# First feed-forward of a two-layer block: gates spread by DMA through DRAM instead of by matmul, and the front of a pair two pairs ahead

## The reference, cut to what matters

```python
xn = _layernorm(x)
gates = softmax(xt @ Wg.T)                       # 16 experts
scores, inds = top_k(gates, 2); scores /= scores.sum()
g = einsum('td,ehd->teh', xt, We_gate)           # 64 hidden rows per expert
u = einsum('td,ehd->teh', xt, We_up)
h = silu(g) * u
y = sum over the 2 chosen experts of scores * (h @ We_down)
shared = silu(xt @ Ws_gate.T) * (xt @ Ws_up.T) @ Ws_down.T   # 256 hidden rows
y = y + sigmoid(xt @ Wsg.T) * shared
```

## Time and profile before

| | before |
|---|---|
| device time, median of 3 runs | 2905.8 us (2904.94 to 2909.46) |
| device time of the profiled execution | 2909.2 us |
| span of the profiled execution | 2907.5 us |
| busy over the span: PE, DVE, ACT, POOL | 90%, 66%, 55%, 21% |
| feed-forward of layer 0, first hidden matmul to last PE work | 42.69 to 554.04 us (the last down matmuls start at 549.92 and take 4.12) |
| mean granted TensorE clock | 0.969 |

### The profile page before, as it was taken

The page is one execution under the profiler, slowest core; times in us unless marked ns, Lnnn a source line. Parts: engine busy times, 40 slices in busy tenths (PEclk is TensorE's granted clock), DMA queues, the critical chain, the costliest instruction groups (busy, mean ns, idle before and its releaser), DMA issues. The chain is left out here.

```text
span 2907.5 us, 102728 instructions
## 1 busy us (share of the span) xinstructions
PE 2604.1 (90%) x42000; PEld 1971.0 (68%) x42000; DVE 1924.4 (66%) x7310; ACT 1611.4 (55%) x3731; POOL 613.6 (21%) x632
## 2 busy tenths in 40 slices
PE   4999999799988999999999999499989999998998
PEld 3777777567767777777777777377766666666666
DVE  4887788467777777777777777211117777777777
ACT  1444444366666666666666665133327666767776
POOL 2445444300110000001111111400004223322230
PEclk9999999899999999999999999699999999999999
DMA  3212100166666666666666665222321001111110
GB/s 131 103 51 73 37 15 12 36 152 148 154 151 149 152 153 148 152 155 149 152 150 153 150 149 123 86 84 98 101 72 35 24 24 29 26 24 24 28 27 9
DMA packets 341502, 268.43 MB, mean 92 GB/s; under 512 B 24602, under 2 KB 328090, under 8 KB 339516
## 3 DMA queue, kind: packets, MB, share of 16 engines
q1 hardware_dynamic: 330556, 234.82, 31.4%
q0 software_dynamic: 10496, 27.28, 3.2%
HBM read 129.88 MB, written 132.14 MB: 90 GB/s over the span
## 5 line engine op out<-in xcount | busy, mean ns | idle before, releaser
L869 DVE CUSTOM_DVE_ANT_0 neg_scores<-scores,rel_bias 128x256 f32<-128x256 f32 x1024 | 373.4, 421 | 271.7 <-PE scores L1013 226.4
L1388 ACT ACTIVATE probs<-neg_scores,low 128x256 f32<-128x256 f32 (+1 forms) x1024 | 382.5, 446 | 211.6 <-DVE low L1419 187.4
L757 ACT ACTIVATE probs<-neg_scores,low 128x256 f32<-128x256 f32 x1024 | 436.8, 500 | 42.9 <-DVE low L869 41.8
L751 ACT COPY probsT_s<-probsT 128x512 f32<-128x512 f32 x256 | 150.3, 587 | 427.6 <-PE probsT L1025 427.6
L1419 DVE CUSTOM_DVE_ANT_0 neg_scores<-scores,alibi 128x256 f32<-128x256 f32 (+1 forms) x1024 | 304.8, 354 | 109.5 <-PE scores L1466 109.2
L1025 PE MATMUL probsT<-consts,probs 128*128 128x128 f32 x2048 | 332.7, 286 | 1.3 <-ACT probsT_s L751 0.7
L1025 PEld LDWEIGHTS probsT<-consts,probs 128*128 128x128 f32 x2048 | 229.1, 143 | 72.9 <-issue 59.4
L252 POOL TENSOR_TENSOR hid<-hid,gate_bc 128x512 f32<-128x512 f32 x160 | 205.4, 1284 | 275.8 <-DVE hid L407 257.3
L876 DVE COPY rel_s<-scores 128x768 f32<-128x768 f32 x256 | 244.0, 953 | 3.0 <-PE scores L1013 1.6
L1003 PE MATMUL scores<-k_sides,q_heads 32*128 32x256 f32 x2048 | 184.3, 429 | 55.6 <-DVE rel_s L876 54.1
L1478 PE MATMUL probsT<-consts,probs 128*128 128x128 f32 x1536 | 226.8, 285 | 3.7 <-ACT probs L1388 0.4
(11 more groups left out here) (187 smaller groups left out, 5158.9 us busy)
## 6 DMA issues: line engine op xcount, KB each, us to landing
rel_rows<-rel_s SPq DMA_DIRECT2D x256, 192.0 KB
rel_bias<-rel_rows SPq DMA_DIRECT2D x256, 192.0 KB, 4.0
rel_rows<-rel_s SPq DMA_DIRECT2D x256, 128.0 KB
rel_bias<-rel_rows SPq DMA_DIRECT2D x256, 128.0 KB, 3.4
packed<-ffn_in SPq DMA_DIRECT2D x8, 1280.0 KB, 5.5
xe<-packed SPq DMA_DIRECT2D x16, 640.0 KB, 4.3
expert_out<-ye POOLq DMA_DIRECT2D x16, 640.0 KB, 6.9
xt<-xnT SPq DMA_DIRECT2D x64, 128.0 KB, 3.1
```

The costliest lines, as they stand in the source:

```text
L757: act.activation(probs[s % 2][:, j, :], neg[s % 2][:, j, :], ACT.Exp, bias=low[s % 3][:, j:j + 1], scale=-1.0).then_inc(exped, 1)
L869: dve.tensor_tensor_reduce(neg[s % 2][:, j, :], S_ps[:, 512 * j:512 * j + S], bias_of(s)[:, j, :], 1.0, 3e38, ALU.add, ALU.min, low[s % 3] ...
L1388: act.activation(probs[s % 3][:, j, 0:w], neg[s % 3][:, j, 0:w], ACT.Exp, bias=low[s % 3][:, j:j + 1], scale=-1.0).then_inc(exped, 1)
```

## The change

It does four things. (1) The matmuls of `spread_gate`, their bank and ACT's copies of it go. Instead ACT copies the transposed gates (17 x 512) to SBUF, SP stores them to DRAM (`gate_rows`, 34 KB) and three DMAs read them back with repeated source rows into `gate_bc`, now 128 partitions x 9 x 512 with two buffers. (2) The gates are no longer split in two parts, the factor 0.5 moves into `gate_values`, and DVE loses two instructions for each pair and one at the start. (3) The front is made for pair p+2 during pair p (AHEAD = 2), so the fronts of pairs 0 and 1 both lie ahead of the first hidden chunk; xnT_parts gets a third buffer. (4) Within a pair the pieces of the front move to earlier steps: on PE 4, 6, 9 become 3, 4, 7; on ACT 4, 8, 9 become 3, 5, 7; on DVE top_two and gate_values move from 7, 8 to 5, 6 (the norm stays at 0, 1, 2); on POOL the subtract moves from 5 to 4.

```diff
+        gate_rows = nc.dram_tensor("gate_rows", (E + 1, 512), F32).ap()
+            AHEAD = 2
-            B_ps = bank_a("gate_spread")
-            xnT2 = [sa(f"xnT_parts{i}", [P, 2, W]) for i in range(2)]
+            xnT2 = [sa(f"xnT_parts{i}", [P, 2, W]) for i in range(3)]
-            gate_bc = [sa(f"gate_bc_{i}", [P, W]) for i in range(3)]
+            gate_bc = [sa(f"gate_bc_{i}", [P, NCHUNK + 1, W]) for i in range(2)]
-            LOADS = 16 * 8
+            LOADS = 16 * 7
             @block.sync
-                sp.dma_start(spread_f[:, :], io["spread"]).then_inc(load_sem, 16)
+                def broadcast_gates(p):
+                    sp.wait_ge(gatesT_moved, p + 1)
+                    if p >= 1:
+                        sp.wait_ge(gate_in[(p - 1) % 2], 48 * ((p - 1) // 2 + 1))
+                    sp.dma_start(gate_rows, gatesT[:, :]).then_inc(gatesT_stored, 16)
+                    sp.wait_ge(gatesT_stored, 16 * (p + 1))
+                    if p >= 2:
+                        sp.wait_ge(hid_done, NK * (p - 1))
+                    to, each = gate_bc[p % 2], P // 2
+                    for half in range(2):
+                        sp.dma_start(to[each * half:each * half + each, 0:NCHUNK, :],
+                                     bass.AP(tensor=gate_rows.tensor, offset=W * half, ap=[[0, each], [2 * W, NCHUNK], [1, W]])
+                                     ).then_inc(gate_in[p % 2], 16)
+                    sp.dma_start(to[:, NCHUNK, :], bass.AP(tensor=gate_rows.tensor, offset=W * E, ap=[[0, P], [1, W]])
+                                 ).then_inc(gate_in[p % 2], 16)
...
                     sp.dma_start(xnT0[2 * p:2 * p + 2].rearrange("b p s -> p b s"),
                                  xnT[p % 2][:, :].rearrange("p (b s) -> p b s", b=2)).then_inc(stored[p % 2], 16)
+                    broadcast_gates(p)
             @block.gpsimd
-                for p in range(-1, NP):
+                for p in range(-AHEAD, NP):
...
-                            pool.wait_ge(gate_moved, m + 1)
-                            pool.tensor_tensor(hid[p % 2][:, k, :], hid[p % 2][:, k, :], gate_bc[m % 3][:, :], ALU.mult).then_inc(hid_done, 1)
+                            if k == 0:
+                                pool.wait_ge(gate_in[p % 2], 48 * (p // 2 + 1))
+                            pool.tensor_tensor(hid[p % 2][:, k, :], hid[p % 2][:, k, :], gate_bc[p % 2][:, min(k, NCHUNK), :],
+                                               ALU.mult).then_inc(hid_done, 1)
             @block.scalar
-                            if k <= NCHUNK:
-                                m = (NCHUNK + 1) * p + k
-                                act.wait_ge(spread_full, m + 1)
...
-                                act.copy(gate_bc[m % 3][:, :], B_ps[:, :]).then_inc(gate_moved, 1)
-                            if k == 4:
-                                act.wait_ge(turned, p + 2)
+                            if k == 3:
+                                act.wait_ge(turned, new + 1)
...
-                            if k == 8:
-                                act.wait_ge(gap_done, p + 2)
+                            if k == 5:
+                                act.wait_ge(gap_done, new + 1)
             @block.vector
                 def gate_values(p):
...
-                    link(dve.tensor_tensor(gates[:, :, 0:E], oh[:, :, 0, :], oh[:, :, 1, :], ALU.add))
-                    if p >= 1:
-                        dve.wait_ge(gatesT_ready, p)
-                    link(dve.tensor_copy(gates2[:, :, 0, :].bitcast(F32R), gates[:, :, :]))
-                    dve.tensor_tensor(gates2[:, :, 1, :].bitcast(F32R), gates[:, :, :], gates2[:, :, 0, :],
-                                      ALU.subtract).then_inc(gates_done, 1)
+                    dve.tensor_tensor(gates[:, :, 0:E], oh[:, :, 0, :], oh[:, :, 1, :], ALU.add).then_inc(gates_done, 1)
                 def prepare():
-                    dve.tensor_copy(spread[:, :].bitcast(F32R), spread_f[:, :])
...
                             if k == 2:
                                 newton()
-                                normal_end(p + 1)
+                                normal_end(new)
-                            if k == 7:
-                                top_two(p + 1)
-                            if k == 8:
-                                gate_values(p + 1)
+                            if k == 5:
+                                top_two(new)
+                            if k == 6:
+                                gate_values(new)
             @block.tensor
                 def front(p, k):
-                    if k == 4:
+                    if k == 3:
                         pe.wait_ge(xn_done, p + 1)
...
-                    if k == 6:
+                    if k == 4:
                         pe.wait_ge(xnT_moved, p + 1)
...
-                    if k == 9:
+                    if k == 7:
                         pe.wait_ge(gates_done, p + 1)
...
-                for p in range(-1, NP + 1):
+                for p in range(-AHEAD, NP + 1):
                     for k in range(NK if p < NP else LAG):
                         if 0 <= p < NP:
                             up(p, k)
-                            if k <= NCHUNK:
-                                spread_gate(p, k)
...
-                        if p + 1 < NP:
-                            front(p + 1, k)
+                        if p + AHEAD < NP:
+                            front(p + AHEAD, k)
```

More of the change, by code:

```diff
@@ L142, in program @@
             hid = [sa(f"hid_{i}", [P, NK, W]) for i in range(2)]
-            gate_bc = [sa(f"gate_bc_{i}", [P, W]) for i in range(3)]
+            gate_bc = [sa(f"gate_bc_{i}", [P, NCHUNK + 1, W]) for i in range(2)]
             gates = sa("gates", [P, TP, NG])
-            gates2 = sa("gates2", [P, TP, 2, NG])
-            gatesT = [sa(f"gatesT_{i}", [2 * NG, W]) for i in range(2)]
+            gatesT = sa("gatesT", [NG, W])
             stats = sa("stats", [P, TP, 6])
@@ L186, in program @@
             hid_raw = sema("hidden_ready")
-            spread_full = sema("gate_spread_ready")
-            gate_moved = sema("gate_spread_moved")
+            gatesT_stored = sema("gatesT_stored")
+            gate_in = [sema(f"gate_in{i}") for i in range(2)]
             hid_done = sema("hidden_gated")
@@ L283, in _ @@
-                        if p + 1 < NP:
-                            new = (p + 1) % 2
-                            if k == 4:
-                                act.wait_ge(turned, p + 2)
[L287 to L294, removed]
-                            if k == 8:
-                                act.wait_ge(gap_done, p + 2)
+                        new = p + AHEAD
@@ new lines, in _ @@
+                        if new < NP:
+                            if k == 3:
+                                act.wait_ge(turned, new + 1)
+                                if new >= 2:
+                                    act.wait_ge(stored[new % 2], 16 * (new // 2))
+                                    act.wait_ge(parts_done, new - 1)
+                                act.copy(xnT[new % 2][:, :], M_ps[:, :]).then_inc(xnT_moved, 1)
+                                if new >= 3:
+                                    act.wait_ge(u_full, NK * (new - 2))
+                                act.wait_ge(xnT_moved, new + 1)
+                                act.copy(xnT2[new % 3][:, 0, :].bitcast(F32R), xnT[new % 2][:, :]).then_inc(upper_done, 1)
+                            if k == 5:
+                                act.wait_ge(gap_done, new + 1)
@@ L297, in _ @@
                                 act.activation(ex[:, :], gap[:, :], ACT.Exp)
                                 act.activation(sg[:, :], logit[:, :, E], ACT.Tanh, scale=0.5).then_inc(ex_done, 1)
-                            if k == 9:
-                                act.wait_ge(gatesT_ready, p + 2)
-                                act.copy(gatesT[new][:, :].bitcast(F32R), M_ps[0:2 * NG, :]).then_inc(gatesT_moved, 1)
+                            if k == 7:
+                                act.wait_ge(gatesT_ready, new + 1)
+                                if new >= 1:
+                                    act.wait_ge(gatesT_stored, 16 * new)
+                                act.copy(gatesT[:, :], M_ps[0:NG, :]).then_inc(gatesT_moved, 1)
@@ L358, in gate_values @@
                     dve.wait_ge(ex_done, p + 1)
-                    dve.tensor_scalar(gates[:, :, E], sg[:, :], 0.5, 0.5, ALU.mult, ALU.add)
-                    link(dve.tensor_scalar(den[:, :], ex[:, :], 1.0, None, ALU.add))
+                    if p >= 1:
+                        dve.wait_ge(gatesT_ready, p)
+                    dve.tensor_scalar(gates[:, :, E], sg[:, :], 0.25, 0.25, ALU.mult, ALU.add)
+                    link(dve.tensor_scalar(den[:, :], ex[:, :], 2.0, 2.0, ALU.mult, ALU.add))
                     link(dve.reciprocal(gk[:, :, 0], den[:, :]))
@@ L407, in _ @@
```

(9 more changed lines are left out.)

42 lines of the change are left out of this document (12 added, 30 removed).

## The result

The change makes the kernel slightly slower: 2904.5 us before (median of 8 runs, 2901.8 to 2909.5) and 2912.0 after (8 runs, 2909.3 to 2916.9), a ratio of 1.0024, 95% interval 1.0013 to 1.0035. The forecast was +18.4 us, the measurement +7.5: direction and mechanism held, the size did not. In the feed-forward both traces agree: a pair takes 32.8 us after the change and took 31.6 before, and the stage ends 4.4 and 2.3 us later. The time lies at the lower end of my own case (2909 to 2945).

A forecast was written before the change was run, and what follows sets the result against it. PE was taken to bound the feed-forward, with DVE next. Start, pairs and end gave 87.4 + 13 x 33.4 + 47.8 = 569.4 against 551.0 us, +18.4, so 2924 us; range 2885 to 2948.

The forecast's parts named there:

- my own case: Feed-forward: two PE stands and clock falls bring 32.2 to 35 us a pair, 2909 to 2945 us; chance 0.55.
- The stand at the transposes (3.1) and at the gates (1.9): In each pair PE waits for DVE's xn 3.1 us and for DVE's gates 1.9 us.
- What the change removes, 4.8 us a pair: On PE, nine spreads a pair at 2.92 - 2.39 = 0.53 us: 4.8 of 31.6 us.
- Full-clock pair, 30.5: A feed-forward pair without clock falls takes 30.5 us against 31.6; two PE stands take 3.7 of the 4.8 us.
- The clock, 2.9 us a pair: Falls to 1.2 GHz behind PE's stands cost 2.0 us (first) and 0.9 (second), making a pair 33.4 us.
- The start: Two fronts precede pair 0: first matmul at 52.9 instead of 42.69, pair 0 takes 34.5 us, pair 1 begins at 87.4.
- The last two pairs: Pairs 14 and 15 have no front and take 2 x 10 x 2.39 = 47.8 us.
- Sum: Start, 13 pairs and last two pairs: 569.4 against 551.0 us, +18.4, program 2924 us.
- The transfers, 0: Gate transfers of 2.36 MB a pair take 7 to 10 us, have some 29, and cost 0.
- POOL never waits for a DMA: Expected sign in the feed-forward: POOL's products never wait for a gate transfer.
- The rival that the clock holds: PE's stands come without clock falls: 30.5 us a pair, -19 us, 2887; chance 0.2.

The follow-up runs named there:

- old step numbers: The changed kernel with the front's pieces at the steps of before, two pairs ahead and gates by transfer kept; ratio 0.9862 to the kernel before, -42.6 us.
- only the first stand left: The changed kernel plus 6 unused matmuls ahead of the gates' transposes, filling the second stand; ratio 1.0001 to the kernel before, +1.4 us.
- Changed again: The changed kernel itself, run once more in another group on its own chip; ratio 0.9971 to the kernel before.
- without the transfers: The changed kernel without the gate broadcasts of pairs 2 to 15, which use the gates of pairs 0 and 1; ratio 1.0005.
- the kernel before with only part 4: The kernel before, spreads and one pair ahead kept, with only the new step numbers; ratio 1.0013 to the kernel before.
- better order: The changed kernel with Newton steps together, transposes at 4, router 5, top_two 6, gate_values 8, gates' transposes in next pair's step 0; ratios 0.969 and 0.9746.
- with the stands filled: The changed kernel plus unused matmuls, 12 ahead of the transposes of xn and 6 ahead of the gates'; ratio 0.9905 to the kernel before, -28.8 us.
- the one two pairs ahead: The kernel before, gates spread by matmuls, with the front two pairs ahead and its pieces reordered over the steps; ratio 0.9962, -12.2 us.

## Why the prediction was right in direction and wrong in size

*The stand at the transposes (3.1) and at the gates (1.9)*: right, 3.3 and 2.0, and on the spot (12.64 and 25.25 us into the pair). The old step numbers show that the first comes from the step at which PE asks and not from DVE being slower.

*What the change removes, 4.8 us a pair*: 5.8. I made the step without a spread, 2.39 us, from the 1.47 us of step 9 and the 0.92 of a down product that stands behind a spread. Without a spread in front the next row follows after 0.81 us (110.35 to 111.16 in the changed kernel), and the step is 2.27.

*Full-clock pair, 30.5*: 30.2. The gain that I missed was mostly not to be had: a faster PE reaches its stand earlier and waits longer, so only the steps behind the last stand count, 2 x 0.12 = 0.24 us a pair.

*The clock, 2.9 us a pair*: 2.6 on average. I had charged a fall behind the first stand 9 times in 10 at 2.2 us and one behind the second 55 times in 100 at 1.7, in no relation to each other. In the profiled execution both falls came together, at 4.2 us in all, in 8 of 13 pairs and neither in 5. The size of a fall was right on average: with only the first stand left, pairs lose 1.6 or 2.8 us against 30.2, mean 2.2. The second fall then has 4.2 - 2.8 = 1.4, and 1.6 where it comes alone. The Trainium skill (TensorE: Matmul & The Clock Gate, "HAM oscillation — how this bites in real kernels") has every turn of its loop start cold; the waits of that loop are given as about 3 to 5 us. Where only the first stand is left, the trace agrees, a loss in each of the pairs 1 to 13; with both stands 5 of 13 pairs have none, which it does not.

*Together* the pairs give 13 x (33.4 - 32.8) = 7.7 us of the error, half from the clean pair and half from the falls.

*The start*: the first hidden matmul came at 51.1, not 52.9, and pair 0 took 32.2 us, not 34.5: -4.1 us. Changed again and without the transfers, pair 0 takes 32.2 and 32.5 us (48.95 to 81.10, 50.16 to 82.70). The 37.3 us of the kernel before, from which I went, were a long case: there the matmuls of the first steps ran at half speed until about 61 us, that is for some 18 us with PE busy, and in the changed kernel only until 53.6, for 2.4. First the kernel before:

```profile
58.72 1.63 PE L464 MATMUL gate_up<-xnT_parts,ffn 128*128 128x512 f32 x3
63.34 0.93 PE L464 MATMUL gate_up<-xnT_parts,ffn 128*128 128x512 f32 x3
```

and the kernel before with only part 4, where they are fast from 2.7 us on and pair 1 begins at 76.32 instead of 79.96:

```profile
42.14 1.63 PE L464 MATMUL gate_up<-xnT_parts,ffn 128*128 128x512 f32 x3
45.35 0.96 PE L464 MATMUL gate_up<-xnT_parts,ffn 128*128 128x512 f32 x3
```

The better order, traced twice, had 8.6 and 3.3 us of it, with pair 0 at 28.1 and 28.3. So this length changes between executions of one kernel, and a few us of pair 0 of the kernel before may belong to the one execution that was profiled; that is argued, since there is only one trace of it.

*The last two pairs*: 558.46 - 509.82 = 48.6 us with the last down products, which the sum left out on both sides. Before, from 522.36, pair 15 took 554.04 - 522.36 = 31.7 us to the same point and 28.7 in the sum, so 3.0 lie in these products, and 45.6 remain of my 47.8: -2.2 us, again the 2.39.

*Sum*: -4.1 - 7.7 - 2.2 = -14.0 against 18.4, that is +4.4, as the stage's end shows. The mechanism held; the terms that failed are these sizes, all of them too long: the pair at 33.4 us measured 32.8 (30.2 for 30.5 at full clock, 2.6 for 2.9 of falls), pair 0 at 34.5 measured 32.2, the first hidden matmul at 52.9 came at 51.1, and the step without a spread at 2.39 measured 2.27, which is in the pair and in the last two. The forecast was the small difference of a gain and three losses, counted 13 times; 0.6 us a pair, 2% of it, makes two fifths of the forecast 18.4. That the direction came out right on such a sum owes something to luck: on the second chip the ratio is below 1.

*The transfers, 0*: right for pairs 2 to 15, by the run without them. *POOL never waits for a DMA*: wrong by one wait, 9.7 us at 56.74, near the 57 of the text; the down product that needs it comes three steps later. *The rival that the clock holds* is in part what happened, in 5 of 13 pairs; with the stands filled, so that it holds everywhere, the program gains 28.8 us, where this rival had 19.

*The step outside the sum*: the stand before the next stage grew from 3.25 to 5.35 us, behind the load of xt, though the order around it is the same. It is 3.2 to 3.3 us in all three kernels with spreads, the one two pairs ahead among them, and 3.6 to 5.4 in the ten traces without, 4.1 where the changed kernel ran again and 4.9 without the transfers. So neither the look-ahead alone nor the 2.36 MB of each pair from 2 on is its cause; what is stays open. In the last stage, which gives 4.9 us back, the granted clock fell 18 times for 3.4 us before and 16 times after. At 1.6 us each (an estimate, from the falls behind the gates' stand) that would be 3.2 of the 4.9; it was not tried.

## What to carry to other kernels

When work is taken off the engine that bounds a loop, ask first where that engine will arrive earlier at a fixed wait: here the same change gained 43 us with the old step numbers, 75 to 86 with better ones, and lost 7, or on another chip stayed level, with the ones that it came with. Moving the askers earlier in the same edit as making them faster counts twice. A stand that costs little in itself can cost more through the clock, and matmuls without use in the gap tell the two apart in one run.

## What the runs showed of the hardware

Whether a stand of 3.3 us is followed by a fall changes between pairs that are alike in work and order: with both stands, three traces (the changed kernel twice, and without transfers) each have falls behind both in 8 of 13 pairs and behind neither in 5. Stands by themselves, the other one filled down to 0.6 us: 2.0 us, a fall in 4 of 13 pairs, 3.4 us long; 3.3 us, in 13 of 13, 6.8 and 3.4 us long in turn. Stands of 0.8 and 0.6, and of 1.23, brought none. With the old step numbers the stand of 2.0 us brought a fall of 3.4 us at half clock 6 times, and such a pair was only 0.7 us longer than the others (29.55 against 28.9), not 1.4 to 1.6: the next wait for DVE's hid took up the rest. That last reason is argued from the 14.5 us of such waits, not tried.

From the first hidden matmul on, with PE at work, the matmuls of the start ran at half speed for some 18 us in the one trace of the kernel before, and for 8.6 and 3.3 us in two traces of one and the same kernel.
